# Edge rows in SBUF at a pitch of 264 words, loaded pair by pair

## The reference

```
def _L1_gnn_ref(x, edge_index, edge_attr, W1, b1, W2, b2):
    ...
    row = edge_index[0]
    col = edge_index[1]
    msg = jnp.concatenate([x[row], x[col], edge_attr], axis=-1)
    h = jax.nn.relu(msg @ W1 + b1)
    msg_out = h @ W2 + b2
    out = jax.ops.segment_sum(msg_out, row, num_segments=x.shape[0])
    return out
```

## Time and profile before

| | |
|---|---|
| median of 3 runs | 5703.44 us |
| profiled execution, own time | 5709.14 us |
| its span, first to last instruction | 5707.3 us |
| PE busy | 5097.3 us (89%) |
| DVE busy | 3955.6 us (69%) |
| POOL busy | 3878.4 us (68%) |
| ACT busy | 2972.5 us (52%) |
| DMA queue q1 (SP's), packets | 662496 |
| DMA queue q0 (POOL's), packets | 190592 |

### The profile page before, as it was taken

One profiled execution on the slowest core, in us unless ns is written; L12 is line 12 of the kernel. 1 busy time (PEld: TensorE's weight loads), 2 busy tenths in 40 slices (PEclk: granted clock), 3 DMA queues, 4 the chain that ended last, 5 costly groups with the idle time before them and its releaser, 6 DMA issues.

```text
span 5707.3 us, 159502 instructions
## 1 busy us (share of the span) xinstructions
PE 5097.3 (89%) x33692; PEld 4028.8 (71%) x33693; DVE 3955.6 (69%) x14408; ACT 2972.5 (52%) x8485; POOL 3878.4 (68%) x3713
## 2 busy tenths in 40 slices
PE   4888888888888885999999999999997999999999
PEld 3677777767777774677666666666665787777877
DVE  6778878878887886455555555555545888888887
ACT  3566666666666653333333333333223777777776
POOL 4777777777777774677777777777776555555553
PEclk6888888898888887999999999999998999999999
DMA  4522222222222234999999899998886999999997
GB/s 109 163 53 54 52 53 54 53 53 53 53 54 53 54 105 135 268 271 268 263 261 261 255 265 264 260 260 260 258 256 191 216 221 219 215 217 218 220 218 191
DMA packets 859992, 990.85 MB, mean 174 GB/s; under 512 B 307993, under 2 KB 663225, under 8 KB 859776
## 3 DMA queue, kind: packets, MB, share of 16 engines
q1 hardware_dynamic: 662496, 608.23, 41.0%
q0 software_dynamic: 190592, 378.22, 24.7%
q10 hardware_dynamic: 6816, 3.38, 0.2%
HBM read 726.65 MB, written 262.76 MB: 173 GB/s over the span
## 4 chain that ended last, share of the span: by engine, by line
PE 56%; DMA 11%; issue 11%; POOL 9%; DVE 8%; DVEq 3%; ACT 2%; POOLq 0%; ACTq 0%; SPq 0%
PE bank L1705 12%; PE bank L1538 10%; PE bank L1628 9%; PE bank L1630 7%; PE bank L1695 7%; DMA xr<-arena 6%; POOL xr L547 5%; POOL arena L499 4%; PE bank L1464 2%; DMA arena<-h_tab,arena 2%; DVE arena L1055 2%; DVE arena L945 2%; PE bank L1618 2%; DMA arena<-p_tab,arena 1%; PE bank L1686 1%
## 5 line engine op out<-in xcount | busy, mean ns | idle before, releaser
L499 POOL DMA_INDIRECT arena<-h_tab,arena x1612 | 1564.3, 970 | 549.2 <-issue 407.6
L547 POOL DMA_INDIRECT xr<-arena x1612 | 1569.6, 974 | 515.4 <-issue 341.6
L1538 PE MATMUL bank<-arena 128*128 128x136 f32 x6448 | 1314.0, 332 | 72.7 <-DVE arena L1055 8.4
L719 ACT ACTIVATE arena<-bank 128x256 f32<-128x256 f32 x1612 | 593.5, 385 | 1393.6 <-PE bank L1630 944.5
L1628 PE MATMUL bank<-arena 128*128 128x256 f32 x3224 | 1031.4, 402 | 82.6 <-DVE arena L1251 44.1
L561 POOL DMA_INDIRECT arena<-p_tab,arena x428 | 669.7, 1565 | 630.9 <-DMA arena<-p_tab,arena 527.0
L1538 PEld LDWEIGHTS bank<-arena 128*128 128x128 f32 x6448 | 983.7, 215 | 158.1 <-DVE arena L1055 62.0
L626 ACT ACTIVATE arena<-bank 128x256 bf16<-128x256 bf16 x1612 | 613.6, 381 | 806.0 <-PE bank L1464 725.1
L1630 PE MATMUL bank<-arena 128*128 128x256 f32 x3224 | 977.1, 385 | 0.0
L1705 PE MATMUL bank<-arena 128*128 128x257 f32 x3424 | 898.5, 384 | 7.0 <-issue 4.9
L1055 DVE TENSOR_TENSOR arena<-arena,bank 128x272 f32 x1612 | 693.5, 430 | 183.5 <-PE bank L1538 152.4
(11 more groups left out here) (255 smaller groups left out, 6550.6 us busy)
## 6 DMA issues: line engine op xcount, KB each, us to landing
arena<-xr SPq DMA_DIRECT2D x428, 516.0 KB, 3.9
arena<-q_tab SPq DMA_DIRECT2D x1612, 128.0 KB
arena<-in_edge_attr SPq DMA_DIRECT2D x61, 832.0 KB
arena<-rel_tab SPq DMA_DIRECT2D x124, 224.0 KB
arena<-h_tab,arena POOLq DMA_INDIRECT x1612
xr<-arena POOLq DMA_INDIRECT x1612
arena<-rel_tab SPq DMA_DIRECT2D x124, 192.0 KB
xr<-arena SPq DMA_DIRECT2D x26, 516.0 KB
```

The lines of the kernel that those rows point to most:

```text
L499: pool.indirect_dma_start(G[:, q, t, :], None, h_tab, bass.IndirectOffsetOnAxis(ap=idx[:, q, t:t + 1], axis=0)).then_inc(sem(f"gath{q}"), 16)
L547: pool.indirect_dma_start(xr, bass.IndirectOffsetOnAxis(ap=pos[:, q, t:t + 1], axis=0), Rb[:, t, :], None).then_inc(sem(f"scat{m}"), 16)
L1538: last = pe.matmul(PSB[3 + t % 2][:, k * H * MW:(k + 1) * H * MW], OH[:, (t + 2 * q) % 4, k * P:(k + 1) * P], flat(msg[:, t, :, :]), start ...
```

## The change

Each row of a pair gets a place of XP = 264 words in `XR`, of which 258 are filled, so the destination of a load is no longer one run per pair and partition but two. A chunk is loaded by two DMAs, one per pair, on the same semaphore, and DVE waits for both. The columns that DVE and POOL address move with the pitch. As `XR` grows from 4128 to 4224 words, `OHq` moves to the next region, behind `sidx`.

```
+XP = HID + 8
...
-        XR, OHp, OHq = S([NS, CP, PR * RW]), S([SB, PR, P]), S([4, PR, P], BF16)
+        XR, OHp = S([NS, CP, PR * XP]), S([SB, PR, P])
...
-        sidx = S([NS, CP], I32)
+        sidx, OHq = S([NS, CP], I32), S([4, PR, P], BF16)
...
-                sp.dma_start(XR[:, s, :, :], xr[bass.ds(c * (CP * GR), CP * GR), :].rearrange("(k p j) w -> p k (j w)", p=P, j=PR)).then_inc(sem(f"xr_in{s}"), 16)
+                for k in range(CP):
+                    sp.dma_start(XR[:, s, k, :].rearrange("p (j w) -> p j w", j=PR)[:, :, 0:RW],
+                                 xr[bass.ds(c * (CP * GR) + k * GR, GR), :].rearrange("(p j) w -> p j w", j=PR)).then_inc(sem(f"xr_in{s}"), 16)
...
-                    pool.indirect_dma_start(XR[:, s, k, RW:RW + HID], None, p_tab,
+                    pool.indirect_dma_start(XR[:, s, k, XP:XP + HID], None, p_tab,
...
-                    dve.wait_ge(sem(f"xr_in{s}"), 16 * (i + 1))
+                    dve.wait_ge(sem(f"xr_in{s}"), 16 * CP * (i + 1))
...
-                    V.tensor_scalar(sidx[:, s, CP - n:], XR[:, s, CP - n:, RW + HID + 1], 0.0, None, ALU.max).then_inc(sem("idx_ready"), 1)
+                    V.tensor_scalar(sidx[:, s, CP - n:], XR[:, s, CP - n:, XP + HID + 1], 0.0, None, ALU.max).then_inc(sem("idx_ready"), 1)
...
-                    c, direct = j * RW + HID, j and added(s, k)
+                    c, direct = j * XP + HID, j and added(s, k)
```

## The result

The changed kernel takes 5827.72 us (median of 4 runs, 5821.49 to 5833.05) against 5703.51 us of the kernel before, measured beside it: a ratio of 1.0219, with a 95% interval of 1.0205 to 1.0233. It is **slower by 124 us**. The direction was forecast, the size was not: 5725 us was the forecast, and 5827.72 lies above the range's end of 5775.

The account below looks back on a forecast made before the run. The source stage's load-to-ReLU loop, 5.9 to 6.0 us a turn, was taken to lead slightly over PE's 5.78. Shorter pieces +22 us, other terms 0, gave 5731 us on the profiled execution, 5725 for the median; range 5680 to 5775.

Parts of the forecast that it names:

- What bounds the kernel: Source stage: load, one-hots, addition and ReLU loop slightly slower than PE; load time counts half per chunk where DVE waits.
- Shorter pieces: Edge-row loads: 1032-byte pieces instead of 2064 add 0.12 us per load, taken as 22 us in all.
- A second issue: SP's second load per chunk, issued 0.53 us behind the first, does not delay the landing: cost 0.
- the cover: DMA engines: the first half's 0.76 us outlasts the 0.53 us issue gap, by a thin 0.23 us.
- The gather's place: POOL's gather writes at offset 1056 bytes, not 1032; same bytes, 0.84 us per engine unchanged: 0.
- sign of a wrong zero: Zero terms are wrong if gathers change their 0.84 us, or ReLU and addition change their widths' times.
- The pitch: ReLU and addition read across an 8-word gap instead of 2; their 630 and 543 ns stay: 0.
- Rival 1: Source-stage loads: each half pays its own start, 68 to 113 us slower, 5793 us; chance 0.08.
- Rival 3: Source-stage loads: shorter pieces are held up less, landing 0.17 us sooner, 22 us faster, 5681 us; chance 0.20.

Follow-up runs that it names:

- e6: Changed kernel, but one load per chunk, four 1032-byte rows per partition at the 264-word pitch, rows 128 apart in HBM: 5705.61 us, ratio 0.9993.
- e12: Kernel before, one load per chunk at the old pitch, but a partition's four rows side by side in SBUF lie 128 rows apart in HBM: 5704.21 us.
- e5: Changed kernel, still two loads per chunk in 1032-byte pieces, but a partition's two rows lie 128 rows apart in HBM: 5773.7 us, ratio 1.0122.
- e1: Kernel before, but each chunk loaded by two DMAs of one pair each, in 2064-byte runs at the old pitch: 5747.08 us, ratio 1.0075.
- e2: Changed kernel, but one load per chunk, four 1032-byte rows per partition side by side in HBM, pairs mixed: 5820.25 us, ratio 1.0201.

## Why the prediction was wrong in size

- *What bounds the kernel.* Right as to the loop that a longer load would make lead, too simple as to the kernel before. The chain of the whole source stage runs through loads for 3.6% of it before and 24.5% after: before, PE and the loop were nearly tied, and a wait of DVE did not yet mean that the loop led. A load's time does count at about half its size: 0.70 / 2 = 0.35 us per chunk, where 0.298 was measured; that PE hid the rest is likely, not shown. Also right: DVE waits more often, 333 times.
- *Shorter pieces, +0.12 us per load.* Too high, if anything. e6 and e12 move twice the pieces, land at 4.02 and 4.03 us in the median for 4.02, and their time does not differ from before. (In halves, e5's short pieces cost 21 us more than e1's long ones, 4.45 against 4.35 us from the first issue to the last landing; 0.04 us of that is the longer issue, the rest is open.) The Trainium skill ("DMA: Bandwidth & Descriptors", section "Specifications") puts line rate at 512 bytes and up; the trace agrees in e6 and e12, and its result, no change, was the right one for this term.
- *A second issue, cost 0, 0.53 us behind the first.* **This step failed twice.** The issue, and with it the start, was taken from the old form's 372 ns; the new form's takes 543 ns, the halves go out 0.74 us apart, and the first data come 0.3 us later. And the cover failed: that the first half would keep the engines busy until the second was queued did not help, as a half takes 3.98 us. Even long runs in two halves (e1) cost 46 us, and two halves of the quick form (e5) 67. The Trainium skill's rule for one large transfer (same page, "Rules for kernel authors") was the better guide here. The two failures do not add up: the slow form in one load costs 119 us (e2), in two, as the changed kernel has it, 124.
- *The gather's place, 0.* The place costs nothing (e6), but the gather's company does: 0.24 us of the slow form's own lateness became 0.71 beside gathers. The prediction had the 0.84 us per engine in its rows and treated it as a fixed neighbour. Its own sign of a wrong zero came: in the changed kernel a gather takes 27.4% x 1395.6 / 421 = 0.91 us of each engine.
- *The pitch, 0.* Right: ReLU keeps 630 ns, and e6 has the pitch and the time of before.
- *Rivals.* Rival 1 described the mechanism best, each half paying its own start, and got a chance of 0.08 and 5793 us. It left out the longer issue and the gathers. Rival 3, shorter pieces held up less, did not occur.

Two things stay open: why a DMA with one HBM run per partition and gaps in SBUF issues and starts later, and which packets of a gather delay which load.

## What to carry to other kernels

Where a loop waits for a load, price the load by its time from issue to landing and not by its bytes; here, beside gathers, a half load took as long as a whole one, and splitting it put the second issue into the loop. Before giving rows a pitch in SBUF, look at the issue's duration in the trace of the new form: rows that lie side by side in HBM and apart in SBUF issued in 543 ns and started 0.3 us later, while the same rows taken 128 apart in HBM cost nothing. A transfer that just fits beside another queue's gathers has no slack to lose: 0.24 us of lateness became 0.71.

## What was not expected of the hardware

- The issue's duration went by the form, not by the number of pieces: 543 ns for 256 pieces and for 512 of one HBM run cut in SBUF, 373 ns for 512 pieces with the rows apart, and 333 ns for one run of 2064 bytes on both sides.
- Pieces of 1032 bytes and of 2064 bytes gave the same time in one load per chunk (5705.61 and 5704.21 us against 5706.44 and 5707.23).
- A load of unchanged form, held back by 0.32 us, took 4.49 us in the median instead of 4.02 beside gathers; without gathers it took 3.65 us held or not, and the hold cost nothing measurable (5633.31 against 5632.5 us).
